# Layer 0 of a two-layer graph network: two matrix products on halves of the TensorE array, and V weighted out of PSUM

## Chip, cores and metric

The kernel runs on one core of one Trainium2 chip. The metric is the device time of one execution in microseconds (us). A core has TensorE (PE in the profile, with its weight loads as PEld), VectorE (DVE), ScalarE (ACT), GpSimd (POOL) and SyncE (SP, which issues most DMAs). All data are float32.

## The reference, cut to what matters

There are 12,500 nodes with 128 features, and 212,500 edges sorted by destination. Layer 0 is edge attention with 8 heads of 16 features; layer 1 is a second attention layer and two dense layers. The change touches layer 0 alone:

```
Q, K, V = x @ WQ, x @ WK, x @ WV ;  Eh = edge_attr @ WE          # heads of 16
score = K[src] * Q[dst] / sqrt(16) * Eh
score = exp(clip(score.sum(-1), -5, 5))                           # one per edge and head
wV = segment_sum(V[src] * score, dst) ;  Z = segment_sum(score, dst)
h = x + wV / (Z + 1e-6)                                           # then batch norm
```

## The kernel before, in words

Edges are handled in 416 chunks of 512 (`NC` = 416, `CE` = 512), each as `K` = 4 slots of 128 edges, one edge per partition. The destinations of a chunk lie in a window of `W` = 64 nodes that begins at the chunk's base. Every engine has its own program for layer 0 inside `edges0`, and semaphores join them; the order on an engine is the order in which the code is written. For chunk c:

- POOL (`gather`, L393) fetches K and V of the sources with four indirect DMAs of 128 rows into `kv_g`, whose 8 buffers (`U` = 8) let it run up to 8 chunks ahead. It waits on `summed`, that is, until PE has used chunk c-8.
- SP loads into 4 buffers each `local` (the chunk's destinations less the base, copied to 64 partitions), `eat` (edge attributes, transposed) and `qw` (the 64 rows of Q in the window); it waits on `turned` for each chunk.
- PE, `spread_out` (L438, L442): Eh = `eat` x WE, and the Q row of each edge as a product of a one-hot matrix `hott` (64 nodes x 512 edges) with `qw`; the sum runs over 64 partitions. Both land in PSUM (`ps_pair`). `sum_up` (L452): the sums per node, as one-hot `hot` (128 edges x 64 nodes) times the weighted V and the weights, 4 slots into one `ps_sum` of 64 partitions. `turn_sums` (L460, L461): turns these sums by a product with the identity into `ps_turn`. On PE the order is `sum_up(c)`, `spread_out(c+2)`, `turn_sums(c)`. Each float32 product appears as two passes in the profile, so four products are "x8".
- DVE: `attend` (L563, L566 products, L568 reduce, L571 clip), `one_hot` (L547), `one_hot_turned` (L555), `value` (L576: V times its weight, in place in `kv_g`), `add_up` (L586: into the accumulator `acc`).
- ACT: `keep_sums` (L499) copies `ps_sum` to `sums`, `weigh` (L503) writes exp(score) behind V in `kv_g`.

The node numbers 0 to 63 lie in a PSUM bank of their own (`ps_iota`) and are one input of `one_hot`.

Of the kernel before, what the change touches and what calls it, by code (L numbers as in the profile page):

```python
# [168 lines left out]
def at(i, n):  # L169
    return bass.ds(i * n, n)  # L170
# [69 lines left out]
def edges0(nc, m, xk, src_cols, dst_rows, dst_cols, edges, weights, vectors):  # L240

    with ExitStack() as ctx:
# [36 lines left out]
        sums_out, turned = sem("sums_out"), sem("spread_and_turned")  # L279
        gated, scored = sem("gated"), sem("scored")  # L280
        weighed, valued, summed, added = sem("weighed"), sem("valued"), sem("summed"), sem("added")
# [3 lines left out]
        qw = sb("qw", [W, 4, D])  # L285
        local = sb("local", [W, 4, CE])
        line = sb("line", [P, 1])
        kv = sb("kv_g", [P, U, K, ROW0])
        hot = sb("hot", [P, 4, K, W])
        hott = sb("hott", [W, 2, CE])  # L290
        prod = sb("prod", [P, CE])
        score = sb("score", [P, 2, K * H])
        sums = sb("sums", [W, 2, D + H])
        ps_pair = ps("ps_pair", [P, 2, 2, CE])
        ps_eh = ps_pair[:, 0].rearrange("p b (k d) -> p b k d", d=D)
        ps_q = ps_pair[:, 1].rearrange("p b (k d) -> p b k d", d=D)
        ps_sum = ps("ps_sum", [P, 2, CE // 2])
        ps_turn = ps("ps_turn", [P, 2, CE])
        ps_iota = ps("ps_iota", [P, CE])[:, 0:W]
        regs = ctx.enter_context(ExitStack())  # L300
# [3 lines left out]
        def _(sp):  # L304
# [105 lines left out]
        def _(pe):  # L410
# [21 lines left out]
            def spread_out(c, u, first=False):  # L432
                b = u % 2
                pe.wait_ge(edge_in[u % 4], landed(c, u % 4, 16, 4))
                if not first:
                    pe.wait_ge(gated, c - 1 + LEAD)
                for k in range(K):
                    nc.tensor.matmul(ps_eh[:, b, k], eat[:, u % 4, at(k, P)], m["w"][:, WE], start=True, stop=True)  # L438
                pe.wait_ge(window_in[u % 4], landed(c, u % 4, 16, 4))
                pe.wait_ge(hott_ready, c + 1)  # L440
                for k in range(K):
                    mm = nc.tensor.matmul(ps_q[:, b, k], hott[:, b, at(k, P)], qw[:, u % 4], start=True, stop=True)  # L442
                if first:
                    mm.then_inc(turned, 1)

            def sum_up(c, u):
                b = u % 2
                pe.wait_ge(hot_ready, c + 1)
                pe.wait_ge(valued, c + 1)
                pe.wait_ge(sums_out, c - 1 + LEAD)  # L450
                for k in range(K):
                    mm = nc.tensor.matmul(ps_sum[0:W, b, 0:D + H], hot[:, u % 4, k], kv[:, u, k, D:ROW0],  # L452
                                          start=(k == 0), stop=(k == K - 1))
                mm.then_inc(summed, 1)

            def turn_sums(c, u):
                b = u % 2
                pe.wait_ge(sums_out, c + 1 + LEAD)
                pe.wait_ge(added, c - 1 + LEAD)
                nc.tensor.matmul(ps_turn[:, b, 0:W], sums[:, b, 0:D], m["ident"][0:W, 0:W], start=True, stop=True)  # L460
                nc.tensor.matmul(ps_turn[0:H, b, W:2 * W], sums[:, b, D:D + H], m["ident"][0:W, 0:W],  # L461
                                 start=True, stop=True).then_inc(turned, 1)

            spread_out(0, 0, True)
            spread_out(1, 1, True)

# [8 lines left out]
        def _(act):  # L475
# [19 lines left out]
            def keep_sums(c, u):  # L495
                b = u % 2
                act.wait_ge(summed, c + 1 + LEAD)
                act.wait_ge(turned, c - 1 + LEAD)
                nc.scalar.copy(sums[:, b], ps_sum[0:W, b, 0:D + H]).then_inc(sums_out, 1)  # L499
# [14 lines left out]
        def _(dve):  # L514
# [27 lines left out]
            do(nc.vector.memset(ps_turn[:, :, 0:2 * W], 0.0))  # L542
            do(nc.vector.tensor_copy(ps_iota, m["iota"][:]))

            lead(dve, [gated, added], LEAD)
            def one_hot(c, u):
                nc.vector.tensor_tensor(hot[:, u % 4],  # L547
                                        m["dst_local"][:, bass.ds(c, 1), :].rearrange("p a k -> p (a k)")
                                        .unsqueeze(2).to_broadcast([P, K, W]),
                                        ps_iota.unsqueeze(1).to_broadcast([P, K, W]),  # L550
                                        ALU.is_equal).then_inc(hot_ready, 1)

            def one_hot_turned(c, u):
                dve.wait_ge(local_in[u % 4], landed(c, u % 4, 16, 4))
                nc.vector.tensor_scalar(hott[:, u % 2], local[:, u % 4], line[0:W], None, ALU.is_equal).then_inc(hott_ready, 1)  # L555

            def attend(c, u):
                b = u % 2
                short = 16 * (K - -(-LAST // P)) if isinstance(c, int) and c == NC - 1 else 0
                flat = lambda v: v.rearrange("p k d -> p (k d)")  # L560
                dve.wait_ge(turned, c + 1)
                dve.wait_ge(kv_in[u], landed(c, u, 16 * K, U) - short)
                nc.vector.tensor_tensor(prod[:].rearrange("p (k d) -> p k d", d=D), ps_q[:, b],  # L563
                                        kv[:, u, :, 0:D], ALU.mult).then_inc(mult, 1)
                dve.wait_ge(mult, c * 2 + 1)
                nc.vector.tensor_tensor(prod[:], prod[:], flat(ps_eh[:, b]), ALU.mult).then_inc(gated, 1)  # L566
                dve.wait_ge(gated, c + 1 + LEAD)
# [21 lines left out]
            for c in range(3):  # L589
                one_hot(c, c)  # L590
            one_hot_turned(0, 0)
            one_hot_turned(1, 1)
# [1104 lines left out]
```

## Time and profile before

| | |
|---|---|
| time, median of 3 runs | 5763.41 us (5759.13 to 5770.78) |
| span of the profiled execution | 4693.0 us |
| busy share of the span: PE, PEld, DVE, ACT, POOL | 81%, 67%, 67%, 23%, 72% |
| layer 0's chunks | about 127 to 2290 us of the span, 5.20 us per chunk |
| granted TensorE clock there, mean | 0.79 |

The span runs from the first instruction to the last; for the profiled execution no time of its own is listed beside it, and the timed runs are 1070 us longer than it. PE's clock has two levels, shown as 1.0 (2.4 GHz) and 0.5 (1.2 GHz); a mean between them is a mixture. A busy share says little by itself here, since a matmul is recorded with its latency.

### The profile page before, as it was taken

What the parts mean: (1) busy time and instruction counts of PE and PEld (TensorE: products, weight loads), DVE (VectorE), ACT (ScalarE), POOL (GpSimd) and SP (SyncE); (2) the same over time, 40 slices, a digit from 0 to 9 for tenths busy, and PEclk for the clock granted to TensorE, in tenths of its full rate; (3) what the DMA queues carried; (4) which work ended last, traced back from release to release, by engine and by line L of the source; (5) the groups of instructions that cost most, each with busy time, mean ns of one, the idle gap of its engine ahead of it and who ended that gap; (6) DMA issues with size and microseconds to landing.
All of it is one profiled execution on the core that took longest, in us unless ns stands there. A gap on an engine that the chain in (4) does not pass through costs nothing. (4 is left out here: it accounts for less than half of the span.)

```text
span 4693.0 us, 76906 instructions
## 1 busy us (share of the span) xinstructions
PE 3812.3 (81%) x19332; PEld 3161.6 (67%) x19333; DVE 3158.1 (67%) x8279; ACT 1078.1 (23%) x4010; POOL 3369.7 (72%) x3437
## 2 busy tenths in 40 slices
PE   6889899989989988888898977777777777777778
PEld 5777777777778877767567755655555556555555
DVE  1877677677777776777646866666666666666657
ACT  3100010000000000000034433333333333333324
POOL 3677777777777777777557777777777777777752
PEclk9887787787776787888687555555555555555559
DMA  7666665666666666666424322222222222222224
GB/s 279 182 182 184 176 189 176 179 183 181 183 181 182 182 183 174 185 179 183 148 86 97 61 61 61 61 61 61 61 61 61 61 61 60 60 61 61 61 58 154
DMA packets 376029, 593.47 MB, mean 126 GB/s; under 512 B 151298, under 2 KB 204520, under 8 KB 374488
## 3 DMA queue, kind: packets, MB, share of 16 engines
q0 software_dynamic: 132880, 330.18, 27.4%
q1 hardware_dynamic: 241544, 255.24, 18.2%
q10 hardware_dynamic: 1552, 7.43, 0.4%
q8 instruction: 23, 0.38, 0.0%
q14 instruction: 30, 0.24, 0.0%
HBM read 551.16 MB, written 40.54 MB: 126 GB/s over the span
## 5 line engine op out<-in xcount | busy, mean ns | idle before, releaser
L393 POOL DMA_INDIRECT kv_g<-kv_table,idx x1661 | 1678.2, 1010 | 568.0 <-issue 498.7
L1065 POOL DMA_INDIRECT xg<-xl_table,idx x1661 | 1583.0, 953 | 519.3 <-issue 498.6
L1130 PEld LDWEIGHTS ps_sum<-pw,xg 128*128 128x128 f32 x3328 | 740.9, 328 | 165.9 <-DVE pws L1271 165.5
L1130 PE MATMUL ps_sum<-pw,xg 128*128 128x64 f32 x3328 | 819.1, 428 | 4.7 <-DVE pws L1271 2.2
L452 PE MATMUL ps_sum<-kv_g,hot 128*64 128x136 f32 x3328 | 606.6, 339 | 246.8 <-issue 245.8
L1117 PE MATMUL ps_tops<-ident,top 128*64 128x128 f32 x832 | 285.9, 447 | 518.7 <-DVE top L1243 518.4
L452 PEld LDWEIGHTS ps_sum<-kv_g,hot 128*64 128x64 f32 x3328 | 480.9, 167 | 314.9 <-issue 310.2
L438 PE MATMUL ps_pair<-w,eat 128*128 128x128 f32 x3328 | 616.3, 342 | 5.1 <-issue 5.1
L438 PEld LDWEIGHTS ps_pair<-w,eat 128*128 128x128 f32 x3328 | 524.2, 240 | 109.3 <-issue 71.7
L442 PE MATMUL ps_pair<-qw,hott 64*128 64x128 f32 x3328 | 583.9, 326 | 2.9 <-DMA qw<-q_table 2.9
L1229 DVE SCALAR_TENSOR_TENSOR ps_lg<-raw 128x256 f32<-128x256 f32 x416 | 185.3, 445 | 573.4 <-ACT raw L1178 566.7
L1178 ACT ACTIVATE raw<-adw,xg 128x64 f32<-128x64 f32 x1664 | 440.6, 336 | 531.7 <-DMA xg<-xl_table,idx 531.3
L442 PEld LDWEIGHTS ps_pair<-qw,hott 64*128 64x128 f32 x3328 | 492.9, 224 | 66.0 <-issue 27.8
L1117 PEld LDWEIGHTS ps_tops<-ident,top 128*64 128x64 f32 x832 | 119.6, 204 | 589.0 <-DVE top L1243 565.4
L499 ACT COPY sums<-ps_sum 64x136 f32<-64x136 f32 x416 | 110.8, 266 | 1394.8 <-PE ps_sum L452 1390.2
L563 DVE TENSOR_TENSOR prod<-ps_pair,kv_g 128x512 f32<-128x512 f32 x416 | 285.2, 685 | 210.0 <-DMA kv_g<-kv_table,idx 182.2
L586 DVE TENSOR_TENSOR acc<-acc,ps_turn 128x128 f32 x416 | 117.0, 281 | 317.9 <-PE ps_turn L461 313.5
L566 DVE TENSOR_TENSOR prod<-prod,ps_pair 128x512 f32<-128x512 f32 x416 | 286.0, 688 | 14.3
L568 DVE TENSOR_REDUCE score<-prod 128x32 f32<-128x512 f32 x416 | 285.4, 686 | 14.3
L1167 ACT COPY third<-newm 128x64 f32 x416 | 101.9, 245 | 805.0 <-DVE ps_lg L1266 559.4
L1121 PE MATMUL ps_tops<-ident,col 64*128 64x64 f32 x832 | 285.5, 445 | 1.1 <-DVE col L1249 1.1
L576 DVE TENSOR_TENSOR kv_g<-kv_g 128x512 f32<-128x512 f32 x416 | 280.4, 674 | 0.6 <-ACT kv_g L503 0.6
(160 smaller groups left out, 4684.9 us busy)
## 6 DMA issues: line engine op xcount, KB each, us to landing
eat<-in_edges SPq DMA_DIRECT2D x416, 256.0 KB
local<-local_table SPq DMA_DIRECT2D x416, 128.0 KB, 3.8
kv_g<-kv_table,idx POOLq DMA_INDIRECT x1661
xg<-xl_table,idx POOLq DMA_INDIRECT x1661
qw<-q_table SPq DMA_DIRECT2D x416, 32.0 KB
adw<-ad_row SPq DMA_DIRECT2D x416, 32.0 KB, 5.1
kv_table<-kv_out SPq DMA_DIRECT2D x25, 512.0 KB, 2.6
xl_table<-xl SPq DMA_DIRECT2D x25, 264.0 KB, 2.8
```

What stands on the lines that cost most here:

```text
L393: nc.gpsimd.indirect_dma_start(out=kv[:, u, k, 0:2 * D], out_offset=None, in_=m["kv_table"], in_offset=bass.IndirectOffsetOnAxis(ap=idx[:, ...
L438: nc.tensor.matmul(ps_eh[:, b, k], eat[:, u % 4, at(k, P)], m["w"][:, WE], start=True, stop=True)
L442: mm = nc.tensor.matmul(ps_q[:, b, k], hott[:, b, at(k, P)], qw[:, u % 4], start=True, stop=True)
L452: mm = nc.tensor.matmul(ps_sum[0:W, b, 0:D + H], hot[:, u % 4, k], kv[:, u, k, D:ROW0], start=(k == 0), stop=(k == K - 1))
L563: nc.vector.tensor_tensor(prod[:].rearrange("p (k d) -> p k d", d=D), ps_q[:, b], kv[:, u, :, 0:D], ALU.mult).then_inc(mult, 1)
L566: nc.vector.tensor_tensor(prod[:], prod[:], flat(ps_eh[:, b]), ALU.mult).then_inc(gated, 1)
L568: nc.vector.tensor_reduce(score[:, b], prod[:].rearrange("p (h d) -> p h d", d=DH), AX, ALU.add).then_inc(mult, 1)
L1065: nc.gpsimd.indirect_dma_start(out=xg[:, u, k], out_offset=None, in_=m["xl_table"], in_offset=bass.IndirectOffsetOnAxis(ap=idx[:, u // B, ...
L1117: nc.tensor.matmul(ps_top[0:W, u % 2, 0:P], top[:, u % 2], m["ident"][:], start=True, stop=True).then_inc(turned, 1)
L1121: mm = nc.tensor.matmul(ps_max[:, u % 2, 0:W], col[:, u % 2:u % 2 + 1].to_broadcast([W, P]), m["ident"][0:W, 0:W], start=True, stop=True)
L1130: nc.tensor.matmul(ps_sum[:, b, 0:W], xg[:, u, k, 0:D], pw[:, b, k], start=(k == 0), stop=(k == K - 1))
L1178: last = nc.scalar.activation(raw[:, u % 4, k], adw[:, u % U], ACT.Identity, bias=xg[:, u, k, D:D + 1])
```

## The change

1. Q rows: `hott`, `local` and `qw` now use all 128 partitions. Slots 0 and 1 lie in partitions 0 to 63, slots 2 and 3 in partitions 64 to 127, each with its own copy of the Q window. The products of the two halves alternate in PE's program.
2. Sums: slots 0 and 1 are summed into partitions 0 to 63 of `ps_sum`, slots 2 and 3 into partitions 64 to 127, alternating. `turn_sums` multiplies by `halves`, two identities of 64 one above the other, which adds the two halves up.
3. Node numbers are read from SBUF, and `one_hot` becomes four `tensor_scalar` of 128x64 in place of one `tensor_tensor` of 128x256. The turned one-hot is one `tensor_scalar` of 128x256 in place of 64x512.
4. The freed PSUM bank holds a second copy of the attention weights (`ps_weights`), written by a second exp on ACT, and `value` multiplies V by it.
5. SP issues two DMAs each for `local` (1 KB per partition instead of 2 KB) and `qw`.

```diff
-                sp.dma_start(qw[:, u % 4], m["q_table"][bass.ds(base, W), :]).then_inc(window_in[u % 4], 16)
+                for half in range(2):
+                    sp.dma_start(qw[at(half, W), u % 4], m["q_table"][bass.ds(base, W), :]).then_inc(window_in[u % 4], 16)
...
-                sp.dma_start(local[:, u % 4], m["local_table"][bass.ds(c, 1), :].partition_broadcast(W)).then_inc(local_in[u % 4], 16)
+                for half in range(2):
+                    sp.dma_start(local[at(half, W), u % 4], m["local_table"][bass.ds(c, 1), at(half, CE // 2)]
+                                 .partition_broadcast(W)).then_inc(local_in[u % 4], 16)
...
-                for k in range(K):
-                    mm = nc.tensor.matmul(ps_q[:, b, k], hott[:, b, at(k, P)], qw[:, u % 4], start=True, stop=True)
+                for j in range(K // 2):
+                    for half in range(2):
+                        mm = nc.tensor.matmul(ps_q[:, b, half, at(j, D)], hott[at(half, W), b, at(j, P)], qw[at(half, W), u % 4],
+                                              start=True, stop=True)
...
-                    mm = nc.tensor.matmul(ps_sum[0:W, b, 0:D + H], hot[:, u % 4, k], kv[:, u, k, D:ROW0],
-                                          start=(k == 0), stop=(k == K - 1))
+                        mm = nc.tensor.matmul(ps_sum[at(half, W), b, 0:D + H], hot[:, u % 4, half * 2 + j], kv[:, u, half * 2 + j, D:ROW0],
+                                              start=(j == 0), stop=(j == K // 2 - 1))
...
-                nc.tensor.matmul(ps_turn[:, b, 0:W], sums[:, b, 0:D], m["ident"][0:W, 0:W], start=True, stop=True)
+                nc.tensor.matmul(ps_turn[:, b, 0:W], sums[:, b, 0:D], halves[:], start=True, stop=True)
...
-                nc.scalar.activation(kv[:, u, :, 2 * D:ROW0], score[:, u % 2].rearrange("p (k h) -> p k h", h=H),
-                                     ACT.Exp).then_inc(weighed, 1)
+                nc.scalar.activation(kv[:, u, :, 2 * D:ROW0], scores, ACT.Exp)
+                nc.scalar.activation(ps_weights, scores, ACT.Exp).then_inc(weighed, 1)
...
-                nc.vector.tensor_tensor(hot[:, u % 4],
-                                        m["dst_local"][:, bass.ds(c, 1), :].rearrange("p a k -> p (a k)")
-                                        .unsqueeze(2).to_broadcast([P, K, W]),
-                                        ps_iota.unsqueeze(1).to_broadcast([P, K, W]),
-                                        ALU.is_equal).then_inc(hot_ready, 1)
+                for k in range(K):
+                    last = nc.vector.tensor_scalar(hot[:, u % 4, k], m["iota"][:], slots[:, k:k + 1], None, ALU.is_equal)
+                last.then_inc(hot_ready, 1)
...
-                nc.vector.tensor_tensor(values, values, kv[:, u, :, 2 * D:ROW0].unsqueeze(3).to_broadcast([P, K, H, DH]),
+                nc.vector.tensor_tensor(values, values, ps_weights.unsqueeze(3).to_broadcast([P, K, H, DH]),
                                         ALU.mult).then_inc(valued, 1)
```

On DVE, at the start of the loop over chunks, the instructions of one chunk before are these (ISA and REGISTER_ALU are the sequencer's own):

```order
L568 TENSOR_REDUCE score<-prod 128x32
L570 REGISTER_ALU
L571 TENSOR_SCALAR score<-score 128x32
L547 ISA
L547 TENSOR_TENSOR hot<-dst_local,ps_iota 128x256
L554 REGISTER_ALU
L555 TENSOR_SCALAR hott<-local,line 64x512
L576 TENSOR_TENSOR kv_g<-kv_g 128x4x128
```

and in the changed kernel, at the same place:

```order
L583 TENSOR_SCALAR score<-score 128x32
L561 ISA
L561 TENSOR_SCALAR hot<-iota,dst_local 128x64
L561 ISA
L561 TENSOR_SCALAR hot<-iota,dst_local 128x64
L561 ISA
L561 TENSOR_SCALAR hot<-iota,dst_local 128x64
L561 ISA
L561 TENSOR_SCALAR hot<-iota,dst_local 128x64
L565 REGISTER_ALU
L566 TENSOR_SCALAR hott<-local,line 128x256
L588 TENSOR_TENSOR kv_g<-kv_g,ps_weights 128x4x128
```

Between the clip and `value` stand five instructions instead of two, and `value` now reads the weights from PSUM.

On SP, the DMA issues for one chunk (c+4) in the same loop, before:

```order
L321 DMA local<-local_table 64x512
L312 ISA
L312 DMA eat<-in_edges 128x512
L166 ISA
L318 DMA qw<-q_table 64x128
```

and in the changed kernel:

```order
L325 DMA local<-local_table 64x256
L325 ISA
L325 DMA local<-local_table 64x256
L314 ISA
L314 DMA eat<-in_edges 128x512
L166 ISA
L321 DMA qw<-q_table 64x128 x2
```

Three issues become five, and `eat` is now behind two of them.

## Rows read from the trace of the kernel before

**Rows 1.** The page: span and busy time by engine.
```profile
span 4693.0 us, 76906 instructions
PE 3812.3 (81%) x19332; PEld 3161.6 (67%) x19333; DVE 3158.1 (67%) x8279; ACT 1078.1 (23%) x4010; POOL 3369.7 (72%) x3437
```

**Rows 2.** Stretches: layer 0's chunks, a piece at half clock, layer 1.
```profile
core 0: us, PE busy (x) PEld busy (x) DVE busy (x) ACT busy (x) POOL busy (x), PEclk, DMA share, GB/s
127.00:2290.00 2163.00, 1914.86 (x11604) 1646.70 (x11604) 1595.99 (x3313) 204.96 (x828) 1647.74 (x1629) 0.79 0.63 181
1176.00:1223.80 47.80, 47.80 (x203) 41.11 (x202) 27.90 (x58) 3.74 (x15) 36.64 (x37) 0.50 0.57 164
...
2520.00:4560.00 2040.00, 1524.37 (x5820) 1244.38 (x5819) 1333.42 (x4569) 703.87 (x2896) 1525.33 (x1600) 0.50 0.28 60
```

**Rows 3.** Line L393, layer 0's gathers on POOL: durations and a wait.
```profile
L393 POOL DMA_INDIRECT kv_g<-kv_table,idx x1661: 942/946/1784, 81.1 to 2286.1; - x185
...
  PE ps_sum L452: 29.1, 23
```

**Rows 4.** The page's costliest groups: gathers of both layers (busy, mean ns | idle).
```profile
L393 POOL DMA_INDIRECT kv_g<-kv_table,idx x1661 | 1678.2, 1010 | 568.0 <-issue 498.7
L1065 POOL DMA_INDIRECT xg<-xl_table,idx x1661 | 1583.0, 953 | 519.3 <-issue 498.6
```

**Rows 5.** Timeline of one chunk at half clock, POOL and DVE (start, length).
```profile
1203.32 0.94 POOL L393 DMA_INDIRECT kv_g<-kv_table,idx  x1 [0.30 <-issue]
1203.46 0.18 DVE L571 TENSOR_SCALAR score<-score 128x32 f32<-128x32 f32 x1
1203.58 0.42 DVE L547 TENSOR_TENSOR hot<-dst_local,ps_iota 128x256 f32<-128x256 f32 x1
...
1203.92 0.59 DVE L555 TENSOR_SCALAR hott<-local,line 64x512 f32<-64x512 f32 x1
1204.44 0.67 DVE L576 TENSOR_TENSOR kv_g<-kv_g 128x512 f32<-128x512 f32 x1
1204.57 1.36 POOL L393 DMA_INDIRECT kv_g<-kv_table,idx  x1 [0.30 <-issue]
```

**Rows 6.** Timeline of PE alone over the same chunk, half clock.
```profile
1202.89 2.08 PE L438 MATMUL ps_pair<-w,eat 128*128 128x128 f32 x8
1204.89 2.07 PE L442 MATMUL ps_pair<-qw,hott 64*128 64x128 f32 x8
1206.76 0.52 PE L460 MATMUL ps_turn<-ident,sums 64*128 64x64 f32 x2
...
1207.53 2.07 PE L452 MATMUL ps_sum<-kv_g,hot 128*64 128x136 f32 x8
1209.53 0.58 PE L438 MATMUL ps_pair<-w,eat 128*128 128x128 f32 x1
```

**Rows 7.** Timeline of one chunk at full clock, DVE and POOL.
```profile
1248.80 0.67 DVE L576 TENSOR_TENSOR kv_g<-kv_g 128x512 f32<-128x512 f32 x1
1249.30 0.99 POOL L393 DMA_INDIRECT kv_g<-kv_table,idx  x1 [0.30 <-issue]
1249.46 0.29 DVE L586 TENSOR_TENSOR acc<-acc,ps_turn 128x128 f32 x1
1249.67 0.68 DVE L563 TENSOR_TENSOR prod<-ps_pair,kv_g 128x512 f32<-128x512 f32 x1
...
1251.85 1.05 POOL L393 DMA_INDIRECT kv_g<-kv_table,idx  x1 [0.30 <-issue]
...
1252.31 0.47 DVE L555 TENSOR_SCALAR hott<-local,line 64x512 f32<-64x512 f32 x1
...
1253.37 0.29 DVE L586 TENSOR_TENSOR acc<-acc,ps_turn 128x128 f32 x1
```

**Rows 8.** Timeline of SP's queue: two issues in a row.
```profile
1207.78 0.47 SPq L321 DMA_DIRECT2D local<-local_table  x1
1208.43 0.45 SPq L312 DMA_DIRECT2D eat<-in_edges  x1
```

More of the change, by code:

```diff
@@ L284, in edges0 @@
         eat = sb("eat", [P, 4, CE])
-        qw = sb("qw", [W, 4, D])
-        local = sb("local", [W, 4, CE])
-        line = sb("line", [P, 1])
+        qw = sb("qw", [P, 4, D])
+        local = sb("local", [P, 4, CE // 2])
+        line, fold = sb("line", [P, 1]), sb("fold", [P, 1])
+        halves = sb("halves", [P, W])
         kv = sb("kv_g", [P, U, K, ROW0])
         hot = sb("hot", [P, 4, K, W])
-        hott = sb("hott", [W, 2, CE])
+        hott = sb("hott", [P, 2, CE // 2])
         prod = sb("prod", [P, CE])
         score = sb("score", [P, 2, K * H])
-        sums = sb("sums", [W, 2, D + H])
+        sums = sb("sums", [P, 2, D + H])
         ps_pair = ps("ps_pair", [P, 2, 2, CE])
-        ps_eh = ps_pair[:, 0].rearrange("p b (k d) -> p b k d", d=D)
-        ps_q = ps_pair[:, 1].rearrange("p b (k d) -> p b k d", d=D)
+        ps_eh, ps_q = ps_pair[:, :, :, 0:CE // 2], ps_pair[:, :, :, CE // 2:CE]
         ps_sum = ps("ps_sum", [P, 2, CE // 2])
         ps_turn = ps("ps_turn", [P, 2, CE])
-        ps_iota = ps("ps_iota", [P, CE])[:, 0:W]
+        ps_weights = ps("ps_weights", [P, CE])[:, 0:K * H].rearrange("p (k h) -> p k h", h=H)
         regs = ctx.enter_context(ExitStack())
@@ L450, in sum_up @@
                 pe.wait_ge(sums_out, c - 1 + LEAD)
-                for k in range(K):
-                    mm = nc.tensor.matmul(ps_sum[0:W, b, 0:D + H], hot[:, u % 4, k], kv[:, u, k, D:ROW0],
-                                          start=(k == 0), stop=(k == K - 1))
+                for j in range(K // 2):
+                    for half in range(2):
+                        mm = nc.tensor.matmul(ps_sum[at(half, W), b, 0:D + H], hot[:, u % 4, half * 2 + j], kv[:, u, half * 2 + j, D:ROW0],
+                                              start=(j == 0), stop=(j == K // 2 - 1))
                 mm.then_inc(summed, 1)
@@ L459, in turn_sums @@
                 pe.wait_ge(added, c - 1 + LEAD)
-                nc.tensor.matmul(ps_turn[:, b, 0:W], sums[:, b, 0:D], m["ident"][0:W, 0:W], start=True, stop=True)
-                nc.tensor.matmul(ps_turn[0:H, b, W:2 * W], sums[:, b, D:D + H], m["ident"][0:W, 0:W],
+                nc.tensor.matmul(ps_turn[:, b, 0:W], sums[:, b, 0:D], halves[:], start=True, stop=True)
+                nc.tensor.matmul(ps_turn[0:H, b, W:2 * W], sums[:, b, D:D + H], halves[:],
                                  start=True, stop=True).then_inc(turned, 1)
+            pe.wait_ge(halves_made, 1)
             spread_out(0, 0, True)
@@ L498, in keep_sums @@
                 act.wait_ge(turned, c - 1 + LEAD)
-                nc.scalar.copy(sums[:, b], ps_sum[0:W, b, 0:D + H]).then_inc(sums_out, 1)
+                nc.scalar.copy(sums[:, b], ps_sum[:, b, 0:D + H]).then_inc(sums_out, 1)
             def weigh(c, u):
                 act.wait_ge(scored, c + 1)
-                nc.scalar.activation(kv[:, u, :, 2 * D:ROW0], score[:, u % 2].rearrange("p (k h) -> p k h", h=H),
-                                     ACT.Exp).then_inc(weighed, 1)
+                scores = score[:, u % 2].rearrange("p (k h) -> p k h", h=H)
+                nc.scalar.activation(kv[:, u, :, 2 * D:ROW0], scores, ACT.Exp)
+                nc.scalar.activation(ps_weights, scores, ACT.Exp).then_inc(weighed, 1)
             weigh(0, 0)
@@ L542, in _ @@
             do(nc.vector.memset(ps_turn[:, :, 0:2 * W], 0.0))
-            do(nc.vector.tensor_copy(ps_iota, m["iota"][:]))
+            do(nc.vector.tensor_scalar(fold[:], line[:], W - 0.5, float(W), ALU.is_gt, ALU.mult))
+            nc.vector.tensor_tensor(line[:], line[:], fold[:], ALU.subtract).then_inc(line_split, 1)
+            nc.vector.tensor_tensor(halves[:], m["ident"][:, 0:W], m["ident"][:, W:P], ALU.add).then_inc(halves_made, 1)
             lead(dve, [gated, added], LEAD)
             def one_hot(c, u):
-                nc.vector.tensor_tensor(hot[:, u % 4],
-                                        m["dst_local"][:, bass.ds(c, 1), :].rearrange("p a k -> p (a k)")
-                                        .unsqueeze(2).to_broadcast([P, K, W]),
-                                        ps_iota.unsqueeze(1).to_broadcast([P, K, W]),
-                                        ALU.is_equal).then_inc(hot_ready, 1)
+                slots = m["dst_local"][:, bass.ds(c, 1), :].rearrange("p a k -> p (a k)")
+                for k in range(K):
+                    last = nc.vector.tensor_scalar(hot[:, u % 4, k], m["iota"][:], slots[:, k:k + 1], None, ALU.is_equal)
+                last.then_inc(hot_ready, 1)
             def one_hot_turned(c, u):
-                dve.wait_ge(local_in[u % 4], landed(c, u % 4, 16, 4))
-                nc.vector.tensor_scalar(hott[:, u % 2], local[:, u % 4], line[0:W], None, ALU.is_equal).then_inc(hott_ready, 1)
+                dve.wait_ge(local_in[u % 4], landed(c, u % 4, 32, 4))
+                nc.vector.tensor_scalar(hott[:, u % 2], local[:, u % 4], line[:], None, ALU.is_equal).then_inc(hott_ready, 1)
             def attend(c, u):
```

16 lines of the change are left out of this document (10 added, 6 removed).

## The prediction

> **What bounds the kernel now.** I read the page first. No engine is at its limit over the whole span [rows 1], so I went on by stage. The windows view gives layer 0's 416 chunks 2163 us, 5.20 us each, at a mean clock of 0.79 [rows 2]. Five us per chunk is the pace of one engine: POOL. Its 1661 gathers (four per chunk) have a median of 946 ns, and 0.30 us of issue lies ahead of each (498.7 us in all) [rows 3, 4]. So a chunk cannot take less than 4 x (0.946 + 0.300) = 4.98 us. POOL hardly ever waits for others: 29.1 us for PE in the whole layer [rows 3]. Layer 0 is therefore POOL's 1678.2 us of gathers, 498.7 us of issue and 29.1 us of waiting, 2206 us from the first gather at 81.1 us to the last at 2286.1 us [rows 3, 4].
>
> The average gather takes 1010 ns, not 946 [rows 4]. Where do the 64 ns come from? The timeline shows it. Gathers beside products, reductions or one-hots take 0.94 or 0.95 us; the one that meets `value` takes 1.36 us [rows 5]. It ends 0.82 us after `value` ends (1204.44 + 0.67 = 1205.11; 1204.57 + 1.36 = 1205.93). At full clock `value` (from 1248.80) ends at 1249.47, early in the next gather, which takes 0.99 us and ends at 1250.29, again 0.82 us behind `value` [rows 7]. `value` is the one operation here whose two inputs both lie in SBUF; L563, with one input in PSUM, starts at 1249.67 inside that gather and adds nothing to its length [rows 7]. So a gather that begins while `value` runs waits for its end.
>
> PE is the second limit, and it depends on the clock. At half clock a chunk takes 6.64 us (1202.89 to 1209.53), with PE busy all the time [rows 2, 6]. At full clock it takes 3.91 us (1249.46 to 1253.37) and DVE's chain sets that [rows 7]. POOL, 8 chunks ahead at most, averages over both.
>
> **The change, part by part.**
>
> *`value` from PSUM.* It removes the wait of the gathers. The whole excess is 1678.2 - 1661 x 0.946 = 106.9 us. Bounds: nothing, if the in-place read and write of `kv_g` in SBUF is what holds POOL, and 107 us. L563 speaks against nothing: it too reads `kv_g` and writes SBUF. A small part stays: a gather with `hott` at work from its middle on takes 1.05 us [rows 7], 0.10 too long, though in another phase `hott` cost it nothing (0.94, [rows 5]). I leave 4 us for this, since the new `tensor_scalar` are shorter (below). Gain: 103 us.
>
> *`one_hot` as four `tensor_scalar`, `hott` of half the length.* The nearest rows are the clip, 32 elements in 0.18 us, with the next instruction 0.12 us after its start, and `hott`, 512 elements in 0.47 us [rows 5, 7]. That is 0.0006 us an element, so 64 elements take about 0.20 us, 0.14 from start to start: 0.56 us for four, against 0.34 for L547 (1203.58 to 1203.92, [rows 5]). `hott` shrinks by 256 elements, 0.15 us. With 0.01 for the PSUM input DVE's chain grows by 0.08, to 3.99 us. Some of these will be held up by a gather, as `hott` is in one row, by 0.12 us (0.59 against 0.47, [rows 5, 7]). One or two such meetings per chunk give 4.1 to 4.25 us; if all five met one, 4.6. The cover is POOL's 4.98 us, and it holds at each of these values. Cost: nothing.
>
> *The second exp.* It delays `value`'s release by about the length of an exp. In its cover stand now five instructions of DVE, about 0.9 us; nothing is late.
>
> *The products by halves.* If the two halves run side by side, the two passes of one product still follow each other, so I let 8 passes take the time of 5. At half clock the Q block lasts 1.87 us and the sums 2.00 (1204.89 to 1206.76, 1207.53 to 1209.53, [rows 6]): three eighths of 3.87 is 1.45 us less. Q and `turn_sums` now differ in the rows they use, one more change of shape: 0.13 us at least, as the Eh block, which ends in one, lasts 2.00 and the Q block, which does not, 1.87; 0.3 at most by my reading. I take 6.64 - 1.45 + 0.2 = 5.4 us per chunk at half clock; the ends are 6.9 (no overlap, 0.3 more) and 4.7 (both blocks halved). At full clock PE has slack already. So PE gains over a us a chunk, and this is worth almost nothing: POOL waits for PE 29.1 us in all, and part of that is the wait for the first chunk, which no faster product removes. I count 0, at most 29.
>
> The Trainium skill (TensorEngine Tiling (Array Packing), Theoretical Speedup and Key Properties) gives up to 2x for halves and says that a change of the tiling mode drains the array. By its factor alone the half-clock chunk would be 4.7 us; the sum stays the same, as POOL is the limit either way.
>
> *SP's issues.* Three at 0.65 us apart [rows 8] become five: 3.25 us per chunk, under 4.98 and even under DVE's 3.99. Behind them are `hott` on DVE and PE's products; loads run four chunks ahead. The DMA engines are 0.63 busy [rows 2]; at 181 GB/s a chunk of 5.20 us moves 941 KB, and 32 KB more do not fill them. Cost: nothing.
>
> **Sum.** Measured against the profiled span: 4693 - 103 = 4590 us. The timed median lies 1070 us above the span; I take that part as fixed. So 5763.4 - 103 = **5660 us**, 1.8% less.
>
> **The rivals.**
>
> *A. Forecast: POOL's pace, 4.98 us per chunk.* 5640 to 5680. Chance 0.66.
>
> *B. More than that* (the PE waits go too, or the 1070 us outside the span shrink with it): 5620 to 5640. Chance 0.06.
>
> *C. Partly given back.* DVE's delays pile up, or gathers meet the five `tensor_scalar` more often than I think; at 0.10 us for one gather in each chunk, as in the 1.05 us row [rows 7], 42 us stay: 5700, at worst 5750. Chance 0.08.
>
> *D. No gain.* `value` still holds POOL because it writes SBUF in place, or the time outside the span does not follow: 5752 to 5775. L563's rows speak against it. Chance 0.07.
>
> *E. Slower: a `tensor_scalar` in SBUF holds POOL as `value` does.* Today's loss is 106.9 / 416 = 0.257 us per chunk for an operation of 0.67 us. For a meeting at a random place the loss grows with the square of the held time: (0.67 + 0.13)^2 / (2 x 1.25) = 0.256. A stretch of 0.9 us of `tensor_scalar` gives (1.03)^2 / 2.5 = 0.42 us, 176 us in all: 5763 - 107 + 176 = 5832. It decides once the loss per chunk is over 0.257. Against it: `hott` runs beside a gather of 0.94 us [rows 5], and there it is `hott` that is late. Chance 0.04. The Trainium skill (SBUF — State Buffer, "SBUF: two separate sides") states just this rule: VectorE and GpSimd share a pair of ports by an exclusive lock, which VectorE takes with two SBUF inputs or in a two-port mode, and it speaks of SBUF-to-SBUF fp32 copies starving a gather's descriptors. Its first half agrees with `value`; the second is not what the 0.94 us gather shows.
>
> *F. Slower: the clock stays at its half level.* In layer 1 it does, over 2040 us, with PE busy 75% of the time [rows 2]. With less work on PE this could come to layer 0. At 5.4 us per chunk PE would then be the limit: 416 x 5.4 = 2246 against 2163 us now, 83 more: 5846. With a share h of the chunks at half clock, POOL stays the limit while 5.4 h + 4.0 (1 - h) is under 4.98, h under 0.70, and the kernel is slower than before above 0.86 (5.20). Now half clock holds 0.42 of the time (clock 0.79), a third of the chunks. For it: PE falls to half clock at present too. Against it: in the half-clock stretch PE is busy without a gap and the clock came back [rows 2]; that will be so at 5.4 too. Chance 0.07, and 0.02 for other losses.
>
> **How the numbers follow.** Less than 0.2% (12 us) either way is about what a measurement of this kernel cannot tell from no change. Faster: A, B, C, 0.80. Same: D, 0.07. Slower: E, F and others, 0.13. The range for 8 in 10 takes A, C and most of B: 5625 to 5740. A alone is 5640 to 5680.
>
> **What would show it.** Right: mean gather 946 to 955 ns and none at 1.36 beside `value`; the last layer-0 gather near 2183 us; POOL waiting for PE no more than 30 us; `value` at about 0.68 us; the Q block shorter than 1.87 us at half clock. Wrong: long gathers that remain beside `value` (D) or beside L561 and L566 (E); a clock near 0.5 and POOL waiting for PE (F); no overlap of the halves would make the blocks as long as before and leave the sum as it is.

## The result, and the profile after

| | before | changed |
|---|---|---|
| time, median of 7 runs | 5759.13 us (5747.33 to 5772.34) | 5778.67 us (5775.98 to 5787.66) |
| ratio | | 1.0038 [1.0026, 1.0049] |
| forecast | | 5660 us, range 5625 to 5740 |

The changed kernel is 0.38% slower where 1.8% faster was forecast. Its profiled execution took 5778.31 us. Its page shows the span, the busy times and, per group of instructions, busy time and mean ns, then the idle time just before them:

```profile
span 5776.5 us, 82001 instructions
PE 3719.1 (64%) x19332; PEld 2936.8 (51%) x19333; DVE 3209.3 (56%) x9529; ACT 1082.8 (19%) x4426; POOL 3277.6 (57%) x3437
L398 POOL DMA_INDIRECT kv_g<-kv_table,idx x1661 | 1591.3, 958 | 1175.7 <-issue 537.6
L1078 POOL DMA_INDIRECT xg<-xl_table,idx x1661 | 1577.7, 950 | 1030.8 <-issue 474.9
```

The span and the time differ by 1.8 us. So nothing lies outside the span, and the 1070 us that I had put there must be inside it. The gathers did what was forecast: 1591.3 us instead of 1678.2, mean 958 ns instead of 1010. What grew is POOL's idle time before them, from 568.0 [rows 4] to 1175.7 us. It also grew before layer 1's gathers, which the change does not touch, from 519.3 to 1030.8 us.

The same line by its waits, in the changed kernel (min/median/max ns, start of the first and of the last; then who ended the waits, us and times):

```profile
L398 POOL DMA_INDIRECT kv_g<-kv_table,idx x1661: 940/946/1152, 80.4 to 2806.7; - x185
  issue: 537.6, 1445
  remote: 530.6, 200
  PE ps_sum L460: 67.8, 15
```

The longest gather takes 1152 ns instead of 1784, but the last one begins at 2806.7 us, not at the 2183 that was forecast. A releaser stands here, 200 times and for 530.6 us, that the trace behind the prediction does not have: "remote", an engine released by something that the view finds no instruction for. A piece of the timeline shows what that is (start, length; idle before, releaser):

```profile
1171.96 0.28 PE L469 MATMUL ps_turn<-halves,sums 128*8 128x64 f32 x2
1172.16 0.68 PE L460 MATMUL ps_sum<-kv_g,hot 128*64 128x136 f32 x8
...
1173.90 0.34 PE L448 MATMUL ps_pair<-qw,hott 64*128 64x128 f32 x1
...
1175.34 0.27 PE L448 MATMUL ps_pair<-qw,hott 64*128 64x128 f32 x1 [1.10 <-issue]
...
1176.09 0.69 PE L448 MATMUL ps_pair<-qw,hott 64*128 64x128 f32 x6 [0.48 <-issue]
1176.33 0.27 ACT L508 COPY sums<-ps_sum 128x136 f32<-128x136 f32 x1 [5.92 <-remote]
...
1176.35 0.29 DVE L598 TENSOR_TENSOR acc<-acc,ps_turn 128x128 f32 x1 [4.73 <-remote]
...
1177.09 0.95 POOL L398 DMA_INDIRECT kv_g<-kv_table,idx  x1 [2.72 <-remote]
...
1178.71 0.18 DVE L583 TENSOR_SCALAR score<-score 128x32 f32<-128x32 f32 x1
...
1178.93 0.23 ACT L513 ACTIVATE kv_g<-score 128x32 f32<-128x32 f32 x1 [2.32 <-DVE score L583]
```

PE ends the turning at 1172.24 and the sums at 1172.84. DVE adds the turned sums 4.1 us later (1176.35), ACT copies the sums 3.5 us later (1176.33), and the two start 0.02 us apart; POOL goes on at 1177.09. The signal from DVE's clip (ends 1178.89) to ACT's exp (1178.93) comes in 0.04 us. So, by the records, signals that TensorE gives arrive microseconds late, all together, while those of DVE do not.

Two things in the same rows ask for care. The ends of matmuls in a profile are modelled, so a late signal and products that are really finished later than recorded look the same here. And PE itself halts in that stretch: three passes of the Q block begin at 1173.90, 1175.34 and 1176.09, where such passes elsewhere follow each other at once. Over the layer PE stands idle 191.1 us before passes of that block (L448), and 3.9 us in the same kernel's trace on the other kind of chip (f1_change, below); in the kernel before the two are 14.9 and 2.9 us (L442, e1 and the trace of before). Below, "late" means late against the recorded end, and whether the signal or the work is late stays open.

### The profile page after: what moved, and what is told of

Same layout as the page of the kernel before. It is cut to its first block and busy times, and to the rows that moved or that the text cites. A ratio compares the mean times of both kernels' runs of the same rounds, so it can differ in the third digit from the quotient of the medians.

```text
span 5776.5 us, 82001 instructions
## 1 busy us (share of the span) xinstructions
PE 3719.1 (64%) x19332; PEld 2936.8 (51%) x19333; DVE 3209.3 (56%) x9529; ACT 1082.8 (19%) x4426; POOL 3277.6 (57%) x3437
## 5 line engine op out<-in xcount | busy, mean ns | idle before, releaser
L398 POOL DMA_INDIRECT kv_g<-kv_table,idx x1661 | 1591.3, 958 | 1175.7 <-issue 537.6
L1078 POOL DMA_INDIRECT xg<-xl_table,idx x1661 | 1577.7, 950 | 1030.8 <-issue 474.9
L460 PE MATMUL ps_sum<-kv_g,hot 128*64 128x136 f32 x3328 | 402.7, 380 | 614.7 <-issue 526.5
L443 PE MATMUL ps_pair<-w,eat 128*128 128x128 f32 x3328 | 722.5, 382 | 24.7 <-issue 24.5
L460 PEld LDWEIGHTS ps_sum<-kv_g,hot 128*64 128x64 f32 x3328 | 260.8, 182 | 680.7 <-issue 570.4
L448 PE MATMUL ps_pair<-qw,hott 64*128 64x128 f32 x3328 | 470.1, 383 | 191.1 <-issue 186.3
L448 PEld LDWEIGHTS ps_pair<-qw,hott 64*128 64x128 f32 x3328 | 355.5, 260 | 299.3 <-issue 281.6
L1262 DVE TENSOR_REDUCE col<-ps_tops 64x1 f32<-64x128 f32 x416 | 116.8, 281 | 615.2 <-remote 469.9
L508 ACT COPY sums<-ps_sum 128x136 f32<-128x136 f32 x416 | 113.2, 272 | 1772.0 <-remote 1226.3
L1180 ACT COPY third<-newm 128x64 f32 x416 | 101.9, 245 | 1831.9 <-remote 988.4
L1134 PEld LDWEIGHTS ps_tops<-ident,col 64*128 64x128 f32 x832 | 207.5, 309 | 363.4 <-DVE col L1262 239.1
L1297 DVE TENSOR_TENSOR acc<-acc,ps_sum 128x128 f32 x416 | 117.2, 282 | 478.8 <-remote 433.6
L561 DVE TENSOR_SCALAR hot<-iota,dst_local 128x64 f32<-128x64 f32 x1664 | 314.9, 301 | 0.7 <-issue 0.3
```

Source lines behind the costliest of these rows:

```text
L398: nc.gpsimd.indirect_dma_start(out=kv[:, u, k, 0:2 * D], out_offset=None, in_=m["kv_table"], in_offset=bass.IndirectOffsetOnAxis(ap=idx[:, ...
L443: nc.tensor.matmul(ps_eh[:, b, k // 2, at(k % 2, D)], eat[:, u % 4, at(k, P)], m["w"][:, WE], start=True, stop=True)
L448: mm = nc.tensor.matmul(ps_q[:, b, half, at(j, D)], hott[at(half, W), b, at(j, P)], qw[at(half, W), u % 4], start=True, stop=True)
L460: mm = nc.tensor.matmul(ps_sum[at(half, W), b, 0:D + H], hot[:, u % 4, half * 2 + j], kv[:, u, half * 2 + j, D:ROW0], start=(j == 0), stop ...
L561: last = nc.vector.tensor_scalar(hot[:, u % 4, k], m["iota"][:], slots[:, k:k + 1], None, ALU.is_equal)
L1078: nc.gpsimd.indirect_dma_start(out=xg[:, u, k], out_offset=None, in_=m["xl_table"], in_offset=bass.IndirectOffsetOnAxis(ap=idx[:, u // B, ...
```

## The experiments

Every kernel here computes the whole reference. The kernels of one batch ran on one chip, with the kernel before beside them, and "ratio" is always to that. The five batches ran on five chips, and these are of two kinds: three where the kernel before takes 5688 to 5737 us, two where it takes 4703 to 4705. By its time the chip of the result (5759) is of the first kind, and by its span the one behind the prediction's trace (4693) of the second. No chip was used in two batches, so a lasting trait of the chip and a state at the time of the batch are not told apart; "kind of chip" stands for either.

### Batch 1: which part takes the gain (kernel before: 5688.51 us)

**e1_same**, the kernel before unchanged, for its trace.

> The kernel before, unchanged, for a trace of an execution as long as the timed ones. The trace that the prediction rests on spans 4693 us, the timed runs some 1070 us more. Theory S (signals late): as in the trace of the changed kernel, many waits end only 2 to 3 us after the instruction that should release them has ended, POOL waits for PE several hundred us in layer 0 instead of 29, a gather cycle still takes 1.25 us when nothing holds it, and the span is about 5755 us. Theory G (gathers slow): the 1070 us lie in the gathers themselves, 1.57 us a cycle instead of 1.25, and POOL still hardly waits.

One run, 5687.1 us, and this from its page and the source view of the gathers:

```profile
span 5685.3 us, 76906 instructions
L393 POOL DMA_INDIRECT kv_g<-kv_table,idx x1661 | 1699.4, 1023 | 1022.9 <-issue 457.8
...
L393 POOL DMA_INDIRECT kv_g<-kv_table,idx x1661: 943/949/1835, 79.2 to 2761.6; - x185
  remote: 296.1, 136
  PE ps_sum L452: 230.3, 153
```

The same program as in [rows 1, 3, 4], 992 us longer. The gathers are nearly as long as there (21 us more in all); the idle time before them is 1022.9 us instead of 568.0, and the last gather of layer 0 begins 475 us later. So this was there before the change. POOL's excess waits, 296.1 + 230.3 = 526.4 us against 29.1 [rows 3], say that on this chip POOL is not what sets the pace of layer 0: theory S of the expectation, not G.

The other half of the excess lies in layer 1, whose gathers also keep their length (1583.0 us in [rows 4]):

```profile
L1065 POOL DMA_INDIRECT xg<-xl_table,idx x1661 | 1583.6, 953 | 981.4 <-issue 467.4
```

Its idle time grew by 981.4 - 519.3 = 462.1 us, that of layer 0 by 454.9, together 917 of the 992 us. In layer 1 the granted clock is 0.50 in this trace (3100 to 5560 us) as in that of before [rows 2], so the clock does not make that half. In layer 0 it is 0.68 here (127 to 2765 us) against 0.79; how much of the 475 us that makes was not separated.

The line that receives TensorE's sums shows it best. ACT's copy of them, first in this run, then in the trace of before, the same program:

```profile
L499 ACT COPY sums<-ps_sum x416: 266/266/270, 158.5 to 2792.9; 64x136 f32<-64x136 f32 x139
...
  remote: 999.5, 143
  PE ps_sum L452: 876.8, 209
```

```profile
L499 ACT COPY sums<-ps_sum x416: 266/266/268, 141.0 to 2298.6; 64x136 f32<-64x136 f32 x139
...
  PE ps_sum L452: 1390.2, 414
```

In the second no wait ends in "remote", and the wait views of all traces on that kind have no such row at all, while all those on the first kind do. The trace of e1 holds 32,975 records of semaphores raised, that of before 96,461, for the same 76,906 instructions; so releasers are named from incomplete records on the first kind, and what is firm there are starts, lengths and idle times. These alone say the same: in before and in f1_change (below) each of the 416 copies begins at most 0.13 us after the recorded end of the sums; in e1 155 of them begin over 0.5 us after both that end and ACT's own previous instruction, the latest 7.0 us, 541 us in all. The 416 exps on ACT, which wait for DVE's clip, all begin within 0.04 us of the clip's end or of ACT's previous instruction, in each of the three.

**e2_weights**: only V weighted out of PSUM, the second exp, and the one-hot as four `tensor_scalar`; TensorE and the loads as before.

```diff
-                nc.vector.tensor_tensor(values, values, kv[:, u, :, 2 * D:ROW0].unsqueeze(3).to_broadcast([P, K, H, DH]),
+                nc.vector.tensor_tensor(values, values, ps_weights.unsqueeze(3).to_broadcast([P, K, H, DH]),
```

> Only the VectorE and ScalarE part of the change: second copy of the weights in PSUM, V multiplied from there, one-hot as four tensor_scalar from SBUF; TensorE and loads as before. Theory S: layer 0 waits for late signals, POOL has slack, so shorter gathers give nothing: -20 to +20 us against before, although no gather is longer than 1.1 us. Theory G (POOL is the pace, as predicted): -80 to -105 us.

Measured: 5734.97 us, ratio 1.0077 [1.0053, 1.0100]. Its page and source rows of the gathers:

```profile
L393 POOL DMA_INDIRECT kv_g<-kv_table,idx x1661 | 1620.7, 976 | 1147.6 <-issue 499.1
...
L393 POOL DMA_INDIRECT kv_g<-kv_table,idx x1661: 943/949/1252, 80.7 to 2808.1; - x185
...
  PE ps_sum L452: 427.0, 210
```

It is 46 us slower, outside the ranges of both theories. Against e1, busy time fell by 1699.4 - 1620.7 = 78.7 us, and idle time rose by 1147.6 - 1022.9 = 124.7. The part that shortens the gathers makes the kernel slower here.

**e3_halves**: only TensorE by halves with its loads and the turned one-hot on 128 partitions; one-hot and `value` as before.

```diff
+            do(nc.vector.tensor_copy(ps_iota, m["iota"][:]))
...
-                nc.vector.tensor_tensor(values, values, ps_weights.unsqueeze(3).to_broadcast([P, K, H, DH]),
+                nc.vector.tensor_tensor(values, values, kv[:, u, :, 2 * D:ROW0].unsqueeze(3).to_broadcast([P, K, H, DH]),
```

(against the changed kernel)

> Only the part on TensorE and its loads: Q products and sums on halves, 128-partition hott, doubled loads; one-hot of the node numbers in PSUM and V multiplied in SBUF as before. Theory S with the doubled loads as the cost: +10 to +30 us. Theory G: 0 to -10 us. If TensorE's time is on the path when signals are late, it should gain: -30 us or more.

Measured: 5664.96 us, ratio 0.9958 [0.9940, 0.9976]: 24 us gained on this chip, near the "30 or more" for TensorE's time on the path and far from the other two ranges. Batch 3 runs it again.

**e4_loads**: the kernel before, with the loads doubled as in the change, the second Q window unused.

```diff
-                sp.dma_start(qw[:, u % 4], m["q_table"][bass.ds(base, W), :]).then_inc(window_in[u % 4], 16)
+                for half in range(2):
+                    sp.dma_start(qw[at(half, W), u % 4], m["q_table"][bass.ds(base, W), :]).then_inc(window_in[u % 4], 16)
```

> The kernel before with the doubled loads alone: local as two DMAs of 256 columns each into the same 64 partitions, the Q window twice (the second copy is not used). Theory S with loads as the cost: +15 to +60 us. Theory G: 0.

Measured: 5728.05 us, ratio 1.0061 [1.0039, 1.0083]: 40 us for loads that I had put at nothing.

### Batch 2: the other kind of chip (kernel before: 4703.22 us)

**f1_change**, the changed kernel.

> The changed kernel once more, on the chip of the other runs. If its parts add up (V from PSUM with four tensor_scalar +0.8%, TensorE on halves with its loads -0.4%), it lies 0.2 to 0.5% above the kernel before.

Measured: 4596.24 us, ratio 0.9775 [0.9763, 0.9788], 107 us faster; the expectation had taken the other kind of chip for granted. From its page, from the gathers by source, and layer 0's stretch in the windows view (columns as in [rows 2]):

```profile
span 4593.3 us, 82001 instructions
L398 POOL DMA_INDIRECT kv_g<-kv_table,idx x1661 | 1576.3, 949 | 566.5 <-issue 504.1
...
L398 POOL DMA_INDIRECT kv_g<-kv_table,idx x1661: 940/946/1230, 79.1 to 2182.7; - x185
...
  PE ps_sum L460: 24.2, 6
```

```profile
127.00:2187.00 2060.00, 1568.61 (x11624) 1237.62 (x11624) 1681.90 (x4554) 245.10 (x1245) 1545.75 (x1629) 0.81 0.67 196
```

This is the forecast, step by step: span 4593.3 (4590), mean gather 949 ns (946 to 955), last gather at 2182.7 us (2183), wait for PE 24.2 us (at most 30). Against [rows 4], busy time fell by 101.9 us and idle time by 1.5. On this kind of chip idle time stayed as it was; on the other it took up the gain.

**f2_onehot**: the change with the one-hot as one `tensor_tensor` again, its node numbers from SBUF.

```diff
-                for k in range(K):
-                    last = nc.vector.tensor_scalar(hot[:, u % 4, k], m["iota"][:], slots[:, k:k + 1], None, ALU.is_equal)
+                nc.vector.tensor_tensor(hot[:, u % 4],
...
+                                        ps_iota.unsqueeze(1).to_broadcast([P, K, W]),
+                                        ALU.is_equal).then_inc(hot_ready, 1)
```

> The changed kernel with the one-hot again as one tensor_tensor of 128x256, now from the node numbers in SBUF (two inputs in SBUF). Theory D (in these executions VectorE's chain is on the path, POOL has slack): the chain is 0.2 to 0.3 us a chunk shorter, so 40 to 100 us less than the changed kernel, although gathers get longer again. Theory G (POOL's pace): it is slower than the changed kernel by up to 50 us, since the one-hot now holds the gathers.

Measured: 4603.62 us, ratio 0.9790 [0.9777, 0.9802]; gathers 1582.6 us, mean 953 ns. That is 7 us slower than the change, 0.15%, and the intervals of the two ratios overlap. Two SBUF inputs in this short operation (0.42 us) make the gathers only 6.3 us longer in all.

**f3_actextra**: the kernel before with six copies of one column more per chunk on ACT, whose results nobody reads.

```diff
+                for extra in range(6):
+                    nc.scalar.copy(spare[:, u % 4, extra:extra + 1], m["vec"][:, 0:1])
```

> The kernel before with six further copies of one column on ScalarE in each chunk, behind the exp, on an engine that is idle four fifths of the time. Theory D: 0 to +10 us, they are not on the path. Theory R (every further instruction costs time in these executions, wherever it stands, about 16 ns by the weights part alone): 2,496 more instructions, +25 to +50 us.

Measured: 4707.97 us, ratio 1.0005 [0.9996, 1.0014].

**f4_issues**: the kernel before, `local` and `qw` each as two DMAs of half the partitions, so the issues of the change with no more data.

```diff
+                    sp.dma_start(qw[at(half, W // 2), u % 4], rows[at(half, W // 2), :]).then_inc(window_in[u % 4], 16)
```

> The kernel before with local and the Q window each loaded by two DMAs of half the partitions: as many DMA issues on SyncE as in the changed kernel, but no more bytes and no more packets. If the loads' cost (+35 us in the run with doubled loads) comes from the two further issues: +25 to +45 us. If it comes from the 66,000 further packets: 0 to +8 us.

Measured: 4706.68 us, ratio 1.0007 [0.9997, 1.0018]. Neither costs anything here.

### Batch 3: the same parts on a chip of the first kind (kernel before: 5737.15 us)

> The VectorE and ScalarE part alone once more. Where the kernel before takes about 4700 us (TensorE's signals in time, POOL the pace): -95 to -107 us, all of the gathers' excess. Where it takes about 5700 us (signals late): +45 us as in the first run.

> The TensorE part with its loads alone once more. Where the kernel before takes about 4700 us: -5 to +10 us, since POOL's gathers stay as they are. Where it takes about 5700 us: -24 us as in the first run.

> Six further ScalarE copies per chunk, off the path. At about 4700 us they cost nothing (+5 us, within the interval). Where the kernel before takes about 5700 us: 0 to +10 us if only work on the path of VectorE and TensorE costs; +25 to +50 us if every further instruction costs there.

> The changed kernel with its one-hot as one tensor_tensor with both inputs in SBUF. At about 4700 us: within 10 us of the changed kernel, -95 to -107 against before. At about 5700 us: if VectorE's chain is on the path there, 40 to 100 us less than the changed kernel, so -20 to -80 us against before; if not, +10 to +30 us like the changed kernel.

| kernel | time | ratio | gathers, busy + idle (us) |
|---|---|---|---|
| g1_weights (= e2) | 5778.48 | 1.0074 [1.0056, 1.0091] | 1616.7 + 1167.7 |
| g2_halves (= e3) | 5744.53 | 1.0006 [0.9996, 1.0017] | 1668.9 + 1078.8 |
| g3_actextra (= f3) | 5756.85 | 1.0041 [1.0027, 1.0055] | 1681.5 + 1080.5 |
| g4_onehot (= f2) | 5723.86 | 0.9975 [0.9965, 0.9985] | 1575.3 + 1151.9 |

The loss of the V part is there again. The gain of the halves part is not: 0.9958 on one chip of this kind and 1.0006 on another, so ratios of one pair of kernels differ by up to half a per cent between such chips. Copies on ACT that cost nothing on the other kind cost 20 us here: added work is not covered. And f2's kernel, slower than the change there, is faster than before here.

The difference between these kernels on DVE is the length of its chain for one chunk. After a late signal its next chunk runs with no wait, so it can be read from one `add_up` to the next, in this order: e1 (the kernel before), g1's twin e2, the change, g2's twin e3, and g4:

```profile
1171.44 0.29 DVE L586 TENSOR_TENSOR acc<-acc,ps_turn 128x128 f32 x1 [6.34 <-remote]
...
1175.27 0.27 DVE L586 TENSOR_TENSOR acc<-acc,ps_turn 128x128 f32 x1
```

```profile
1173.56 0.29 DVE L584 TENSOR_TENSOR acc<-acc,ps_turn 128x128 f32 x1 [4.72 <-remote]
...
1176.06 0.74 DVE L548 TENSOR_SCALAR hot<-iota,dst_local 128x64 f32<-128x64 f32 x4
...
1177.71 0.27 DVE L584 TENSOR_TENSOR acc<-acc,ps_turn 128x128 f32 x1
```

```profile
1178.85 0.74 DVE L561 TENSOR_SCALAR hot<-iota,dst_local 128x64 f32<-128x64 f32 x4
1179.51 0.35 DVE L566 TENSOR_SCALAR hott<-local,line 128x256 f32<-128x256 f32 x1
...
1180.37 0.28 DVE L598 TENSOR_TENSOR acc<-acc,ps_turn 128x128 f32 x1
```

```profile
1192.24 0.29 DVE L599 TENSOR_TENSOR acc<-acc,ps_turn 128x128 f32 x1 [4.41 <-remote]
...
1195.93 0.28 DVE L599 TENSOR_TENSOR acc<-acc,ps_turn 128x128 f32 x1
```

```profile
1173.30 0.29 DVE L600 TENSOR_TENSOR acc<-acc,ps_turn 128x128 f32 x1 [5.18 <-remote]
...
1175.79 0.42 DVE L560 TENSOR_TENSOR hot<-dst_local,iota 128x256 f32<-128x256 f32 x1
...
1176.99 0.28 DVE L600 TENSOR_TENSOR acc<-acc,ps_turn 128x128 f32 x1
```

That is 1175.27 - 1171.44 = 3.83 us in the kernel before, 1177.71 - 1173.56 = 4.15 in e2, 1180.37 - 1176.35 = 4.02 in the change, 1195.93 - 1192.24 = 3.69 in e3 and 1176.99 - 1173.30 = 3.69 in g4. (The 3.91 of [rows 7] is of a stretch without late signals.) The ratios on this kind of chip follow that order: 1.0074 and 1.0077 at 4.15, 1.0038 and 1.0017 at 4.02, 1 at 3.83, and 0.9958, 1.0006 and 0.9975 at 3.69, where 1.0006 cannot be told from 1. The size is less than the whole: 0.32 us x 416 = 133 us for e2, 46 measured (5734.97 - 5688.51).

### Batch 4: again on a chip of the second kind (kernel before: 4704.52 us)

> The kernel before with the doubled loads (two issues and 160 further packets a chunk). At about 4700 us: 0, within the interval. At about 5700 us: +35 us as in the first run.

> Two further issues a chunk on SyncE, no further packets. At about 4700 us: +3 us as before. At about 5700 us: half or more of the doubled loads' cost, +15 to +30 us, if each further instruction costs about 10 ns there, as ScalarE's six copies did (2,217 more); 0 to +8 us if the packets are what costs.

> The changed kernel with one-hot as one tensor_tensor from SBUF and with local and the Q window each in one DMA over 128 partitions: 4,700 instructions fewer than the changed kernel, the same packets. At about 4700 us: -95 to -107 us against before. At about 5700 us: -30 to -50 us against before, if the further instructions are what eats the gain there.

> The changed kernel on the chip of the other three. At about 4700 us: -107 us. At about 5700 us: +20 to +25 us as in the measurement of the change.

h1 (= e4): 4710.47 us, 1.0010 [0.9996, 1.0023]. h2 (= f4): 4709.20, 1.0010 [0.9998, 1.0021]. h4, the change: 4598.37, 0.9771 [0.9753, 0.9788]. Loads and issues cost nothing that can be measured here, the change gains as in f1.

h3 is f2 with each pair of loads made one DMA over 128 partitions:

```diff
+                rows = m["q_table"][bass.ds(base, W), :].unsqueeze(0).to_broadcast([2, W, D])
+                sp.dma_start(qw[:, u % 4], rows).then_inc(window_in[u % 4], 16)
...
+                halves_of = m["local_table"][bass.ds(c, 1), :].rearrange("a (h e) -> (a h) e", h=2).unsqueeze(1).to_broadcast([2, W, CE // 2])
+                sp.dma_start(local[:, u % 4], halves_of).then_inc(local_in[u % 4], 16)
```

It took 5295.50 us, ratio 1.1251 [1.1231, 1.1272], where a gain of about 100 us was expected. Its timeline and a row of its page:

```profile
1299.76 0.54 SPq L326 DMA_DIRECT2D local<-local_table  x1
1300.49 2.94 SPq L315 DMA_DIRECT2D eat<-in_edges  x1
```

```profile
L567 DVE TENSOR_SCALAR hott<-local,line 128x256 f32<-128x256 f32 x416 | 152.7, 367 | 1178.6 <-DMA local<-local_table 1178.6
```

The issue behind the broadcast load of `local` takes 2.94 us instead of 0.45 [rows 8] (median over the layer 3.37), and DVE waits for `local` in all 1178.6 us. Two plain issues are far cheaper than this one. As h3 fell on the second kind, its question, whether fewer instructions save time on the first, has no answer.

### Batch 5: issues and the change once more on the first kind (kernel before: 5687.61 us)

> Two further issues a chunk on SyncE, no further packets. At about 4700 us: +5 us, within the interval, as twice before. At about 5700 us: +15 to +30 us if further instructions cost about 10 ns each there; 0 to +8 us if the packets are what costs.

> The changed kernel on the same chip. At about 4700 us: -107 us. At about 5700 us: +15 to +25 us; the sum of its parts there is +45 (V part) and 0 (TensorE part with its loads, mean of -24 and +3 rounded up), so a sum of the parts would give +20 to +45.

i1 (= f4): 5652.66 us, ratio 0.9931 [0.9912, 0.9949]. More issues make the kernel 35 us faster here, while e4's, with more data, made it 40 us slower. So "each instruction more costs a little", from which +15 to +30 us was expected, is wrong for this kind of chip.

i2, the change: 5699.35 us, ratio 1.0017 [1.0007, 1.0027]. The gathers on its page:

```profile
L398 POOL DMA_INDIRECT kv_g<-kv_table,idx x1661 | 1589.8, 957 | 1132.5 <-issue 508.7
```

The kernel before takes the same time on this chip as on that of e1 (5687.61 and 5688.51), so the two traces can be laid side by side: busy 1589.8 - 1699.4 = -109.6 us, idle 1132.5 - 1022.9 = +109.6 us. That the two are equal to a tenth is in part chance: the profiled execution of i2 took 5686.12 us, the shortest of its twelve, where their median is 5699.35.

## Why the prediction was wrong, point by point

**The step that failed** is "The timed median lies 1070 us above the span; I take that part as fixed". On the chips of the result, the time is the span and 1.8 us. The 1070 us are waits inside it: in e1, 992 us longer than the prediction's trace, 917 us are POOL's idle time before its gathers, and TensorE's signals come late by the records. The trace behind the prediction has no such waits. With it falls what the sum rested on: "POOL is the limit". In e1, the kernel before on such a chip, POOL waits 526.4 us for others in layer 0, not 29.1.

**Terms that lost their cover.** Because POOL does not set the pace there, -103 us is worth nothing by itself (i2: -109.6 busy, +109.6 idle), and additions priced "Cost: nothing" cost something. The prediction's "DVE's chain grows by 0.08" was 0.19 behind a late signal (3.83 to 4.02). With the one-hot in one operation again the chain is 3.69 and the ratio 0.9975 (g4), where the change has 1.0017 to 1.0038; these were not measured on one chip, and e3 and g2 show that chips of this kind differ by as much. The loads alone cost 40 us (e4); whether by their data or by the moment at which they fall is open, since as many issues without more data gain 35 (i1). That the longer DVE chain is what costs in e2 and the change is a reading that fits the order above and is not shown: g3, e4 and i1 move the time by -0.7 to +0.6% with that chain as it was (3.83 in each), so it is not the only thing, and no run changed the chain's length alone on one chip. Why the change is 0.2 to 0.4% slower rather than equal stays open.

**Rivals.** None named the cause. D had the nearest words ("the time outside the span does not follow"), at 5752 to 5775 and chance 0.07 (5778.67 measured), but its mechanism is wrong: nothing lies outside the span, and no gather is held by `value`. C is right in kind (given back) and wrong in place: the gathers are short, and what they saved went into waits. E is refuted by f1's mean gather of 949 ns, with 1664 + 416 `tensor_scalar` on DVE beside the gathers. The Trainium skill (SBUF — State Buffer, "SBUF: two separate sides") states such a lock; its half on two SBUF inputs agrees with `value` before the change [rows 5]; by its half on two-port operations, if these `tensor_scalar` run in such a mode, which no record here says, that mean would be longer than it is. F is refuted: the clock in layer 0 was 0.81 in f1, and 0.71 in the changed kernel on the chip of the result (127 to 2810 us), over the 0.68 of e1. Rows of f1 beside `value`:

```profile
1205.86 0.68 DVE L588 TENSOR_TENSOR kv_g<-kv_g,ps_weights 128x512 f32<-128x512 f32 x1
1205.90 0.95 POOL L398 DMA_INDIRECT kv_g<-kv_table,idx  x1 [0.30 <-issue]
```

`value` takes 0.68 us as forecast and the gather that begins 0.04 us after it 0.95, where the one in [rows 5] took 1.36.

**The terms themselves.** Where the trace's kind of chip is measured, the sum holds: -107 us (f1) and -106 (h4) for -103. The four `tensor_scalar` take 0.74 us as a group, 0.66 to the start of the next instruction, where 0.56 was forecast. The halves run beside each other at least as fully as I took ("8 passes take the time of 5"). PE at half clock, in the changed kernel:

```profile
1180.55 1.17 PE L460 MATMUL ps_sum<-kv_g,hot 128*64 128x136 f32 x8 [3.20 <-issue]
1181.66 2.08 PE L443 MATMUL ps_pair<-w,eat 128*128 128x128 f32 x8
1183.66 1.23 PE L448 MATMUL ps_pair<-qw,hott 64*128 64x128 f32 x8
1184.82 0.43 PE L468 MATMUL ps_turn<-halves,sums 128*128 128x64 f32 x2
```

From start to start the sums take 1181.66 - 1180.55 = 1.11 us instead of 2.00 (forecast 1.25), the Q block 1184.82 - 1183.66 = 1.16 instead of 1.87 [rows 6] (forecast 1.17), while the Eh block, not split, takes 2.00 as before. As forecast, this is worth little where POOL sets the pace.

**What stays open.** Why TensorE's signals are late on some chips, whether they or the products behind them are late, and why the time there moves by half a per cent with changes off the path. g4's version beats the kernel before on the one chip of the first kind where it ran (5723.86 against 5737.15); the change did not run there. On the second kind it is 0.979 and the change 0.9775.

## What to carry to other kernels

Before a sum is made against a trace, lay its span beside the timed median; a gap of 20% is not a constant to be carried along but says that the trace is of another situation, and "who sets the pace" must be asked again there. A gain on an engine that other waits slow down anyway can be worth nothing, and work added elsewhere under its cover is then no longer free. So where a stall's place is uncertain, the version that lengthens no engine's chain is the safer guess: here one `tensor_tensor` of 0.42 us in place of four `tensor_scalar` of 0.74 costs 0.15% on the chips of the second kind. On the first kind its ratio is lower by 0.4 to 0.6%, but measured on other chips than the change's, so that gain is not shown.

## What the hardware showed that I had not expected

- The same program takes 4703 to 4705 or 5688 to 5759 us, by the kind of chip. On the slower kind ACT and DVE go on some us after the recorded end of TensorE's products (3.5 and 4.1 in the rows above, ACT idle 999.5 us before its copies on 143 "remote" waits), and on DVE's signals ACT goes on in 0.04 us.
- A 128x512 `tensor_tensor` of DVE with two SBUF inputs delays a gather on POOL (0.82 us between their ends, [rows 5, 7]); with one input in PSUM it does not (0.95 us, f1). One of 128x256 with two SBUF inputs lengthened all gathers together by 6.3 us (f2).
- Float32 products that alternate between halves of the array, by rows or by columns, take 0.56 to 0.62 of the time that they took one after the other (1.11 of 2.00, 1.16 of 1.87).
- A DMA of `local` whose source pattern repeats each of two half rows over 64 partitions (h3) makes the next issue of its queue take 2.94 us instead of 0.45.
